# Scan stage: the step size's sums go from VectorE to GpSimd, the router's exponential goes ahead of a table load, and the scatters are split

## The reference

```python
dt = einsum('blr,dr->bld', dt_low, W_dt)
delta = jax.nn.softplus(dt + b_dt)            # the step size: 256 channels x 512 tokens
A = -exp(A_log)                               # 256 x 16 states
def step(h, inp):                             # over the 512 tokens
    dlt_t, B_t, C_t, x_t = inp
    h = h * exp(dlt_t[:, :, None] * A) + dlt_t[:, :, None] * B_t[:, None, :] * x_t[:, :, None]
    return h, einsum('bdn,bn->bd', h, C_t)
y = (ys + D_param * xT) * silu(z)             # and W_out back to 128 features
# then the last mixture: LayerNorm, softmax over 8 experts, the best 2 of them for each token
```

## Time and profile before

| | |
|---|---|
| median of 3 runs | 3106.44 us (3099.91 to 3107.15) |
| the profiled execution's own time | 3107.2 us |
| its span, first to last instruction | 3105.4 us |
| busy, of the span | PE 79%, DVE 67%, ACT 51%, POOL 54% |
| mean granted TensorE clock | 0.92 |
| scan stage | about 1580 to 2780 us of the span |
| one sequence in its middle | about 71 us |

### The profile page before, as it was taken

The page is one execution under the profiler, slowest core; times in us unless marked ns, Lnnn a source line. Parts: engine busy times, 40 slices in busy tenths (PEclk is TensorE's granted clock), DMA queues, the critical chain, the costliest instruction groups (busy, mean ns, idle before and its releaser), DMA issues. The chain is left out here.

```text
span 3105.4 us, 48513 instructions
## 1 busy us (share of the span) xinstructions
PE 2450.2 (79%) x12848; PEld 1728.6 (56%) x12848; DVE 2065.8 (67%) x6055; ACT 1577.2 (51%) x3073; POOL 1691.7 (54%) x1341
## 2 busy tenths in 40 slices
PE   4239996885699854299978888888888888759994
PEld 3229994664699733299943333333333343339993
DVE  6514445775444355255539999999999999965554
ACT  3115554763355444155546666666566566515551
POOL 5745551455455447555515566776666666654552
PEclk9999997996899976699989999999999999979997
DMA  9137772211677532477723333443434343327777
GB/s 331 54 121 229 225 228 67 68 51 41 191 228 227 162 105 72 120 228 228 228 89 129 128 132 131 145 143 133 138 124 137 123 137 130 130 71 231 225 227 229
DMA packets 266836, 476.35 MB, mean 153 GB/s; under 512 B 37133, under 2 KB 180331, under 8 KB 266576
## 3 DMA queue, kind: packets, MB, share of 16 engines
q1 hardware_dynamic: 223552, 402.51, 42.2%
q0 software_dynamic: 34560, 67.99, 6.1%
q10 hardware_dynamic: 8592, 4.33, 0.5%
HBM read 380.32 MB, written 98.01 MB: 154 GB/s over the span
## 5 line engine op out<-in xcount | busy, mean ns | idle before, releaser
L1748 POOL TENSOR_TENSOR ssm_HC<-ssm_H,ssm_BC 128x1024 f32<-128x1024 f32 x255 | 599.8, 2352 | 415.1 <-DVE ssm_psX L1818 344.3
L1504 PE MATMUL ssm_psY<-ssm_HC,ident 128*128 128x512 f32 x1020 | 523.0, 639 | 112.0 <-POOL ssm_HC L1748 111.9
L1662 ACT ACTIVATE ssm_dA<-ssm_delta,A 128x511 f32<-128x511 f32 x512 | 333.0, 710 | 187.0 <-DVE ssm_H L1827 117.8
L1504 PEld LDWEIGHTS ssm_psY<-ssm_HC,ident 128*128 128x128 f32 x1020 | 191.9, 199 | 381.2 <-issue 190.5
L1825 DVE TENSOR_TENSOR_SCAN ssm_H<-ssm_dA,ssm_psX 128x512 f32<-128x512 f32 x256 | 309.1, 1208 | 0.0
L1827 DVE TENSOR_TENSOR_SCAN ssm_H<-ssm_dA,ssm_psX 128x512 f32<-128x512 f32 x256 | 304.7, 1190 | 0.0
L471 POOL DMA_INDIRECT xslots<-att_r_xn,att_r_idx x128 | 128.8, 1006 | 176.5 <-DVE att_r_idx L451 138.3
L884 POOL DMA_INDIRECT a_back<-a_yr,a_to_row x142 | 137.8, 971 | 149.8 <-DVE a_yr L964 128.2
L884 POOL DMA_INDIRECT b_back<-b_yr,b_to_row x142 | 137.9, 971 | 148.4 <-DVE b_yr L964 126.7
L884 POOL DMA_INDIRECT d_back<-d_yr,d_to_row x142 | 137.8, 971 | 144.7 <-DVE d_yr L964 123.1
L884 POOL DMA_INDIRECT c_back<-c_yr,c_to_row x142 | 137.9, 971 | 143.3 <-DVE c_yr L964 121.6
(11 more groups left out here) (566 smaller groups left out, 5773.2 us busy)
## 6 DMA issues: line engine op xcount, KB each, us to landing
ssm_BC<-bc_rows SPq DMA_DIRECT2D x128, 1024.0 KB
a_W<-in_l_pack SPq DMA_DIRECT2D x71, 514.0 KB
b_W<-in_l_pack SPq DMA_DIRECT2D x71, 514.0 KB
c_W<-in_l_pack SPq DMA_DIRECT2D x71, 514.0 KB
d_W<-in_l_pack SPq DMA_DIRECT2D x71, 514.0 KB
a_xs<-xslots SPq DMA_DIRECT2D x71, 131.0 KB
b_xs<-xslots SPq DMA_DIRECT2D x71, 131.0 KB
c_xs<-xslots SPq DMA_DIRECT2D x71, 131.0 KB
```

The source lines that it names most:

```text
L1504: last = nc.tensor.matmul(psY[:, dt, :], k.ident[:, :], HC[:, n % RP, dt, :], start=(n == 0), stop=(n == NB - 1))
L1662: last = nc.scalar.activation(dA[:, n % RA, dt, 1:], delta[:, b, dt, 1:], ACT.Exp, scale=A[:, dt, n:n + 1])
L1748: nc.gpsimd.tensor_tensor(HC[:, n % RP, :, :], H[:, n % RH, :, :], BC[:, n // CHUNK % SLOTS, 1, n % CHUNK:n % CHUNK + 1, :].to_broadcast([ ...
```

## The change

Five things, all in the order of instructions or in their form:

1. The three sums of the step size are issued by GpSimd: `correct` behind the product of state 11, `lengthen` behind that of 12, `sum_up` (`delta`) behind that of 13. `correct` was one VectorE instruction with two operations; it is split into an ACTIVATE Copy with bias -1 on ScalarE at state 10 and a subtraction on GpSimd. `ux` stays with VectorE after state 15.
2. ScalarE's `act_2` goes ahead of the logarithm and its two table loads.
3. The eight scatters of a sequence are split: four behind the products of states 7 to 10, four behind those of states 0 to 3 of the next sequence.
4. Short VectorE instructions of the form tensor_scalar, and a copy with a cast, become tensor_tensor or scalar_tensor_tensor with a constant tile; this is in every stage with a router. One of them (the mean times 0.5) goes away, folded into later scalars.
5. Four constant tiles of 128 x 16 are filled at the start.

```diff
-        nc.vector.tensor_scalar(m, m, 0.5, None, ALU.mult)
...
-        last = nc.vector.tensor_scalar(w[:, 0, :], v, EPS, None, ALU.add)
+        last = nc.vector.tensor_tensor(w[:, 0, :], v, self.k.eps[:, 0:T], ALU.add)
...
+                act.wait_ge(one_ready, s + 1)
+                nc.scalar.activation(rest[:, :, :], rest[:, :, :], ACT.Copy, bias=-1.0).then_inc(less_ready, 1)
...
+                    if n == (12 if after else 10) and before:
+                        R.act_2(nc, act, s - 1)
                     if n == 12 and after:
                         lengthen(s + 1)
-                    if n == (12 if after else 10) and before:
-                        R.act_2(nc, act, s - 1)
...
+            def correct(s):
+                pool.wait_ge(less_ready, s + 1)
+                nc.gpsimd.tensor_tensor(rest[:, :, :], soft, rest[:, :, :], ALU.subtract).then_inc(rest_ready, 1)
+            def lengthen(s):
+                pool.wait_ge(l_ready, s + 1)
+                pool.wait_ge(rest_ready, s + 1)
+                nc.gpsimd.tensor_tensor(rest[:, :, :], absv, rest[:, :, :], ALU.add).then_inc(sized, 1)
+            def sum_up(s, b):
+                pool.wait_ge(sized, s + 1)
+                pool.wait_ge(v_ready, s + 1)
+                nc.gpsimd.tensor_tensor(delta[:, b, :, :], rest[:, :, :], v[:, :, :], ALU.add).then_inc(delta_ready, 1)
+            correct(0)
+            lengthen(0)
+            sum_up(0, 0)
...
-                    if n >= 8 and there(s - 2):
-                        R.pool_one(pool, s - 2, s % 2, n - 8)
+                    if n < 4 and there(s - 3):
+                        R.pool_one(pool, s - 3, 1 - b, n + 4)
+                    if 7 <= n < 11 and there(s - 2):
+                        R.pool_one(pool, s - 2, b, n - 7)
+                    if n == 11 and after:
+                        correct(s + 1)
+                    if n == 12 and after:
+                        lengthen(s + 1)
+                    if n == 13 and after:
+                        sum_up(s + 1, 1 - b)
```

More of the change, by code:

```diff
@@ L210, in dve_stats @@
         yield from chain.link(nc.vector.tensor_tensor(o, st[:, :, 1], st[:, :, 4], ALU.subtract))
-        nc.vector.tensor_scalar(m, m, 0.5, None, ALU.mult)
         yield from chain.link(nc.vector.scalar_tensor_tensor(out=o, in0=o, scalar=0.25, in1=o, op0=ALU.mult, op1=ALU.mult))
         yield from chain.link(nc.vector.scalar_tensor_tensor(out=v, in0=v, scalar=1.0 / D, in1=o, op0=ALU.mult, op1=ALU.add))
-        last = nc.vector.tensor_scalar(w[:, 0, :], v, EPS, None, ALU.add)
+        last = nc.vector.tensor_tensor(w[:, 0, :], v, self.k.eps[:, 0:T], ALU.add)
         if self.w == 2:
-            last = nc.vector.tensor_scalar(w[:, 1, :], v, 1.0 + EPS, EPS * EPS, ALU.mult, ALU.add)
+            last = nc.vector.scalar_tensor_tensor(out=w[:, 1, :], in0=v, scalar=1.0 + EPS, in1=self.k.eps_eps[:, 0:T], op0=ALU.mult, op1=ALU.add)
         last.then_inc(self.asked, 1)
@@ L341, in dve_0 @@
         if not self.first:
-            yield from chain.link(nc.vector.scalar_tensor_tensor(out=n.back[:, 0:T], in0=n.mean[:, 0:T], scalar=-0.5, in1=n.rstd[:, 0, 0:T], op0=ALU.mult, op1=ALU.mult))
-            last = nc.vector.tensor_scalar(n.rstd[:, 0, 0:T], n.rstd[:, 0, 0:T], 0.5, 1.0, ALU.mult, ALU.add)
+            yield from chain.link(nc.vector.scalar_tensor_tensor(out=n.back[:, 0:T], in0=n.mean[:, 0:T], scalar=-0.25, in1=n.rstd[:, 0, 0:T], op0=ALU.mult, op1=ALU.mult))
+            last = nc.vector.scalar_tensor_tensor(out=n.rstd[:, 0, 0:T], in0=n.rstd[:, 0, 0:T], scalar=0.5, in1=k.ones_row[:, 0:T], op0=ALU.mult, op1=ALU.add)
         last.then_inc(n.scaled, 1)
         self.free(dve, b, turn)
-        nc.vector.tensor_scalar(self.rows(s, b)[:, :, D], k.token[:, bass.ds(t0, T)], 1.0, None, ALU.mult)
+        nc.vector.tensor_tensor(self.rows(s, b)[:, :, D], k.token[:, bass.ds(t0, T)], k.zeros[:, 0:T], ALU.add)
     def act_0(self, nc, act, s, b, turn):
@@ L450, in dve_2c @@
         yield from chain.link(nc.vector.tensor_reduce(row, pos.rearrange("p t (c e) -> p t c e", c=TOPK), AX.X, ALU.add))
-        nc.vector.tensor_copy(self.ids(s, b), row.rearrange("p t c -> p (t c)")).then_inc(self.rowed, 1)
+        nc.vector.tensor_tensor(self.ids(s, b), row.rearrange("p t c -> p (t c)"), k.zeros[:, 0:TOPK * T], ALU.add).then_inc(self.rowed, 1)
     def dve_start(self, nc):
@@ L805, in _ @@
             nc.vector.memset(k.ones[:, :], 1.0)
+            for row, value in ((k.zeros, 0.0), (k.ones_row, 1.0), (k.eps, EPS), (k.eps_eps, EPS * EPS)):
+                nc.vector.memset(row[:, :], value)
             clear_rows(nc, empty[:, :]).then_inc(cleared, 1)
@@ L1741, in _ @@
         def _(pool):
+            def correct(s):
[9 more added lines that the diff above has]
+                nc.gpsimd.tensor_tensor(delta[:, b, :, :], rest[:, :, :], v[:, :, :], ALU.add).then_inc(delta_ready, 1)
             R.pool_start(pool)
+            correct(0)
+            lengthen(0)
+            sum_up(0, 0)
             for s in range(BATCH):
-                for n in range(NB if s < LAST else NB - 1):
+                b, after = s % 2, there(s + 1)
+                for n in range(NB if after else NB - 1):
                     pool.wait_ge(h_ready, s * NB + n + 1)
@@ L1766, in normalize @@
                 N.dve_scales(nc, s).then_inc(N.scaled, 1)
-            def correct(s):
-                dve.wait_ge(one_ready, s + 1)
-                nc.vector.scalar_tensor_tensor(out=rest[:, :, :], in0=rest[:, :, :], scalar=-1.0, in1=soft, op0=ALU.add, op1=ALU.subtract, reverse1=True).then_inc(rest_ready, 1)
-            def lengthen(s):
-                dve.wait_ge(l_ready, s + 1)
-                dve.wait_ge(rest_ready, s + 1)
-                nc.vector.tensor_tensor(rest[:, :, :], absv, rest[:, :, :], ALU.add).then_inc(sized, 1)
             def weigh(s, b):
-                dve.wait_ge(sized, s + 1)
-                dve.wait_ge(v_ready, s + 1)
-                nc.vector.tensor_tensor(delta[:, b, :, :], rest[:, :, :], v[:, :, :], ALU.add).then_inc(delta_ready, 1)
                 dve.wait_ge(delta_ready, s + 1)
@@ L1837, in _ @@
             straight(N.dve_stats(nc, chain, 1), normalize(1))
-            correct(0)
-            lengthen(0)
             weigh(0, 0)
@@ L1861, in _ @@
                         small.begin(R.dve_2a(nc, dve, chain, s - 1, 1 - b))
-                    if n == 13 and after:
-                        correct(s + 1)
-                    if n == 14 and after:
-                        lengthen(s + 1)
                     if n == (13 if after else 11) and before:
@@ L1898, in macaron_kernel @@
         k.token, k.slot = sb("token", [P, TILES]), sb("slot", [P, SPREAD])
+        k.zeros, k.ones_row, k.eps, k.eps_eps = (sb(n, [P, 4 * SEQ_TILES]) for n in ("zeros", "ones_row", "eps", "eps_eps"))
         k.pad_row = sb("pad_row", [P, EXPERTS], I32)
```

9 lines of the change are left out of this document (5 added, 4 removed).

## The result

The changed kernel takes 3085.18 us (median of 4 runs, 3079.44 to 3085.44) against 3106.77 for the kernel before on the same chip: 0.9934 of it, 95% interval 0.9919 to 0.9949. Forecast were 3089 and "faster". The profiled execution took 3085.05 us with a span of 3083.3, 22.1 less than before.

The account below looks back on a forecast made before the run. No engine bounds every stage; in the scan stage VectorE does, 97% busy. Sum: 3107.2 + 2 - 3.4 - 17.5 - 3 + 3.5 = 3089 us; 8-in-10 range 3048 to 3118, likeliest case 3079 to 3100.

Parts of the forecast that it names:

- what GpSimd gets: Scan stage, product 11 to `ux`: 4.21 us leaving VectorE return as 4.25 of waiting; +2 us over 15 sequences (-5 to +14).
- The hold of `ux` by product 14: End of the stretch: product 14 starts right behind `sum_up` and keeps `ux` out 0.15 us more.
- Who gets the next turn: Behind products and sums: waiting L418, L419, L421 get in after one GpSimd instruction each, held 1.2, 1.7, 1.2 us.
- rival 3: Behind product 12 GpSimd goes first, `ux` starts at 41.7: +3 us x 15 = 45, so 3134; chance 0.13.
- my own test: In the changed profile, L418 showing 3 us or more would make the prediction wrong.
- My argument against rival 3: Behind product 12, L1771 and a scatter were both waiting; L1771 went through at once (1.70 us), the scatter after it.
- every input is there in time: GpSimd never waits from product 11 to product 14: seven steps of 2.42 us; logarithm ends about 27.6, `lengthen` comes at 29.
- The clock after state 1: TensorE's gap before the last `total` shrinks to 2.7 us, full clock in part of the sequences: -17.5 us (0 to -23.5).
- The exponential: Router's exponential ahead of the logarithm's table load: VectorE's 3.4 us of waiting over 14 sequences go, -3.4.
- The first sequence: Ahead of the loop, sums and `ux` took 4.89 us; now a ScalarE pass and three GpSimd steps, 8.3: +3.5 us.
- The -3 for the short instruction that went: One short instruction less in each LayerNorm, two a sequence: -2 us; in the routing stages another -1 at most.

Follow-up runs that it names:

- Experiment 2: The changed kernel with all eight scatters back behind products 8 to 15: 3125.82 us, 1.0062 of the kernel before.
- Experiment 1: The kernel before, sums still on VectorE, with four spare matrix products ahead of the last `total`: 3083.19 us, ratio 0.9924.
- experiment 10: The changed kernel with four spare matrix products between the totals of products 14 and 15: 0.9973 of the kernel before.
- Experiment 4: The changed kernel with `act_2` again behind the logarithm and its table loads: 3087.17 us, 0.9936 of the kernel before.
- experiment 6: The changed kernel with the router's choice begun behind `ux` and product 14 waiting for `ux`: 0.9920 of the kernel before.
- 8: The kernel of experiment 6 with `sum_up` moved ahead of product 13, and product 13 waiting for `ux`: 1.0019 of the kernel before.
- 11: The kernel of experiment 6 with no short VectorE instruction in states 0 and 1, four a state from state 2: 1.0013 of the kernel before.

## Why the prediction was right

**What leaves comes back (step "what GpSimd gets").** Right, and the central point: 4.21 us of sums went, and the stretch kept its length: `ux` at 17.46 us behind the scans of state 12, where it was at 17.42. Over 14 sequences that part is -0.3 us, where +2 was forecast. Two errors cancel in it. A step of GpSimd's row takes 2.31 us from start to start and not 2.42, since a product or a sum that follows at once overlaps the end of the one ahead; seven make 16.2. The other 0.8 is the wait of product 13 for `psX`, which came late because L417 was held so long. 7 x 2.42 is 16.9 and 7 x 2.31 + 0.80 is 17.0: that they meet is luck. The hold of `ux` by product 14 (0.15 us forecast) didn't come either; `ux` took 1.20 us.

**Who gets the next turn.** Here the pattern was wrong. I had L418, L419 and L421 (now L417, L418 and L420) held 1.2, 1.7 and 1.2 us, by one instruction each. In 11 of 14 sequences L417 was held 3.3 to 3.6 us, through product 12 and `lengthen`: the first meeting went as rival 3 said, and by my own test ("3 us or more") the forecast's pattern had failed. Only three showed mine (0.7 to 1.4 us, then 1.8 to 2.1, then 1.18). But rival 3 needed VectorE to lose a second time, to product 14, and there it did not: L420 got in behind `sum_up`, and `ux` started on time. Experiment 2, with a hold of 5.33 us and more scatters in the row, has a stretch of 20.43. My argument against rival 3 was one row in which L1771 went ahead of a waiting scatter; a waiting sum behaved otherwise.

Two of the three exceptions have a cause that the rows show. In them ScalarE's logarithm (L1657) ended 0.2 us behind product 12, so that `lengthen` was not ready, and L417 went through in the gap:

```profile
1884.68 1.35 DVE L417 TENSOR_TENSOR ssm_r_work<-ssm_r_prob,ssm_r_pv 128x32 f32<-128x32 f32 x1
1886.26 2.34 POOL L1753 TENSOR_TENSOR ssm_rest<-ssm_pre,ssm_rest 128x1024 f32<-128x1024 f32 x1 [0.27 <-ACT ssm_pre L1657]
```

In the 11 the logarithm had ended 1.2 to 1.5 us before product 12 did. So of the 12 meetings behind product 12 at which both were ready, GpSimd had 11; the one that VectorE had is in the first sequence with a router, where the logarithm ended 0.7 us before. That every input is there in time, as I had it, was thus nearly so. Behind a sum it went the other way: L418 got in behind `lengthen` in those three, and L420 behind `sum_up` in all 14, with a product waiting each time. What decides a turn stays open: in experiment 2 a product did go ahead of L418 behind `lengthen`.

**The clock after state 1.** Right in kind and nearly in size: forecast -17.5 us. The rest fell from 11.44 to 9.98 us on average, -1.46 over 13 sequences, -19.0. But the way there was another. I had the full clock in part of the sequences because the gap shrinks to 2.7 us. What I had left out is a gap of 2.2 to 2.3 us ahead of the `total` of product 12, in 10 of the 13. In seven of them that `total` ran wholly or in part at the low level (2.9 to 3.7 us), TensorE's work behind it came later, and the last gap was 1.2 us or less with 1.98 to 1.99 us behind it. In the other three it took 1.98, the last gap was 2.5, and the last `total` took 2.46 to 2.75, with 0.92 us of wait at `take`:

```profile
2092.47 1.98 PE L1505 MATMUL ssm_psY<-ssm_HC,ident 128*128 128x512 f32 x4 [2.21 <-POOL ssm_HC L1770]
2107.55 2.75 PE L1505 MATMUL ssm_psY<-ssm_HC,ident 128*128 128x512 f32 x4 [2.51 <-POOL ssm_HC L1770]
```

So the low level moved, in half of the sequences, from a `total` that VectorE waits for to one that it doesn't. Ten of 13 last `total` took 1.98 to 1.99 us. Experiment 1 shows that this term by itself is worth the whole gain, and experiment 10 that nothing is left to add to it.

**The exponential.** Forecast -3.4 us; in the stretch -4.0 came, and no sequence has 18.35 any more. But it does not come from the order of `act_2`. Experiment 4 puts that back and loses nothing that can be told. Once GpSimd sets `ux`, a wait ahead of L417 is only taken out of its hold. The number was right, the edit that it was put down to was not.

**The rest.** The first sequence: +3.5 forecast. Its `ux` came 5.7 us later, of which 2.1 stand ahead of the stage's work (the first `ssm_n_newton` at 1587.58, where it was at 1585.46), so 3.5. Not foreseen was the period behind it, 65.81 us before and 60.39 after, -5.4. Of that, 2.5 are in the stretch (16.65 to 14.14), which has no router in it and so no short instruction to be held; but the `ux` at its end was held by product 14 (3.37 us), and that comes back in the period behind it, where it stands in the clock's -19.0. The other 2.9 are a wait at the first `take` of the loop: before, TensorE's `gather` was late for it, and with `ux` 3.5 us later it is not. The first sequence's +3.5 was mostly hidden by that. The row of before that shows `gather` behind the first convolutions, and the one of after:

```profile
1631.00 1.98 PE L583 MATMUL ssm_psR<-ssm_t_rows,ident 128*128 128x512 f32 x4 [0.78 <-ACT ssm_pre L1603]
```

```profile
1633.82 1.98 PE L582 MATMUL ssm_psR<-ssm_t_rows,ident 128*128 128x512 f32 x4 [0.78 <-ACT ssm_pre L1604]
```

`gather` ends 11.1 us behind the start of `ux` before (1621.88) and 8.3 after (1627.54). The -3 for the short instruction that went is at most -1.1, which is what the terms leave over inside the loop; 0.4 of it is the wait at `gated` that went from the last period. The +2.1 and the +2.0 outside the loop are read off and not explained.

The terms, forecast and measured: stretch +2, -0.3; exponential -3.4, -4.0; clock -17.5, -19.0; first period 0, -5.4; short instruction -3, -1.1; first sequence +3.5, +3.5; ahead of the stage's work 0, +2.1; behind the last `ux` 0, +2.0. Together -18.4 and, up to rounding, -22.1.

## What to carry to other kernels

Moving work from VectorE to GpSimd gave nothing by itself here: VectorE's instructions with two SBUF inputs were held beside it, and once they were moved away, `ux` waited for GpSimd's row (experiment 6). So count GpSimd's row from the last point at which it waits, and expect the later engine to take back what was given; a hold shows as busy time on a tiny instruction, not as a wait. Taking a hold away moves it to the next short instruction that meets a product, as experiments 6, 8 and 11 did in turn, so lay out the whole sequence and not only the place of the hold. And look first for the cheap cause: filling the gap of 3.8 us ahead of the last `total`, with three lines, gave as much as the whole change.
